# Gated cross-attention and mixture of experts on one core: new step lists, shifts on VectorE, experts by pairs of token tiles

## The reference

```python
def xattn(q, kv):                       # Wq 256x1024, Wk and Wv 128x1024, Wo 1024x256
    qh, kh, vh = heads(q @ Wq), heads(kv @ Wk), heads(kv @ Wv)
    attn = softmax(einsum('bhnd,bhmd->bhnm', qh, kh) * 64 ** -0.5)
    return merge(einsum('bhnm,bhmd->bhnd', attn, vh)) @ Wo + bo

def ffn(x):
    probs = softmax(x @ gate_w.T)       # 8 experts
    comb = the two largest of probs, zero elsewhere
    return sum over e of (x @ expert_w[e].T + expert_b[e]) * comb[:, e:e + 1]

x = x + tanh(g_xattn) * xattn(layernorm(x), ctx)
x = x + tanh(g_ffn) * ffn(layernorm(x))
```

## Time and profile before

| | us |
|---|---|
| median of three runs | 1087.82 (1087.06 to 1088.49) |
| profiled execution, its own time | 1084.83 |
| its span, first to last instruction | 1083.0 |
| start up to the first maximum | 27.7 |
| first batch | 138.4 |
| six middle batches together | 753.6 |
| last batch and tail | 163.3 |

### The profile page before, as it was taken

How to read it: one execution, slowest core, us unless ns; L and a number is a source line. 1 busy time by engine, 2 the same in 40 slices (tenths; PEclk the granted TensorE clock), 3 DMA queues, 4 the chain that set the end, 5 groups by cost and what they waited for, 6 DMA issues and landing times.

```text
span 1083.0 us, 27288 instructions
## 1 busy us (share of the span) xinstructions
PE 950.4 (88%) x10660; PEld 590.7 (55%) x10660; DVE 828.2 (76%) x1551; ACT 788.8 (73%) x1092; POOL 723.0 (67%) x692
## 2 busy tenths in 40 slices
PE   5767669998998989899898989989898989989998
PEld 4245436655655555565465546555555655555583
DVE  5855647797787967799677968879777986778857
ACT  3678869885898848886698848988588866988620
POOL 3479967866677756867478666777578674787510
PEclk7788989999999989999899989999999999999999
DMA  5568759987798849999498956989599985989720
GB/s 166 153 116 136 136 104 181 166 145 120 121 192 158 155 75 170 151 168 153 78 189 158 151 109 124 188 154 159 84 169 166 160 140 97 183 139 152 134 50 20
DMA packets 549135, 150.87 MB, mean 139 GB/s; under 512 B 537592, under 2 KB 547216, under 8 KB 548752
## 3 DMA queue, kind: packets, MB, share of 16 engines
q1 hardware_dynamic: 549008, 149.13, 78.9%
HBM read 11.70 MB, written 4.19 MB: 15 GB/s over the span
## 4 chain that ended last, share of the span: by engine, by line
POOL 33%; issue 19%; PE 17%; ACT 15%; DVE 13%; DMA 1%; SPq 1%; POOLq 0%; ACTq 0%; DVEq 0%
POOL p_s L584 22%; PE MB L1174 9%; ACT pf L741 6%; ACT p_s L751 5%; DVE nmax L903 4%; PE PV L1337 3%; POOL shifts L575 3%; PE ST L1313 3%; POOL xn L559 2%; POOL x L598 2%; PE MB L1186 2%; DVE acc L861 1%; POOL rstd L542 1%; DVE v_s L895 1%; ACT v_s L673 1%
## 5 line engine op out<-in xcount | busy, mean ns | idle before, releaser
L584 POOL TENSOR_TENSOR p_s<-pf,p_s 128x1024 f16<-128x1024 f32 x254 | 541.5, 2132 | 173.2 <-ACT p_s L751 137.6
L741 ACT ACTIVATE pf<-ST,shifts,s_mul 128x512 f32<-128x512 f32 x512 | 370.7, 778 | 152.0 <-POOL shifts L575 150.8
L903 DVE TENSOR_REDUCE nmax<-ST 128x2 f32<-128x1024 f32 x256 | 309.0, 1216 | 38.8 <-PE ST L1313 36.6
L751 ACT ACTIVATE p_s<-pf 128x1024 f16<-128x1024 f32 x254 | 267.6, 1060 | 3.8
L1337 PEld LDWEIGHTS PV<-v_s,pt_s 128*128 128x128 f16 x6096 | 205.9, 98 | 83.9 <-issue 77.7
L1337 PE MATMUL PV<-v_s,pt_s 128*128 128x65 f16 x6096 | 230.2, 194 | 6.0 <-DVE o_n L921 6.0
L1174 PE MATMUL MB<-ex_s,x2t_s 128*128 128x512 f16 x708 | 179.7, 393 | 0.0
L1313 PE MATMUL ST<-KH,QH 64*128 64x512 f16 x512 | 101.2, 391 | 66.3 <-ACT pf L741 54.7
L575 POOL TENSOR_SCALAR shifts<-nmax,s_mul 128x2 f32<-128x2 f32 x256 | 69.4, 271 | 121.4 <-DVE nmax L903 104.3
L861 DVE SCALAR_TENSOR_TENSOR acc<-MB,m,acc 128x256 f32<-128x256 f32 x236 | 113.8, 482 | 24.2 <-PE MB L1174 17.1
L1174 PEld LDWEIGHTS MB<-ex_s,x2t_s 128*128 128x128 f16 x708 | 67.1, 101 | 73.2 <-issue 10.3
(11 more groups left out here) (156 smaller groups left out, 1035.5 us busy)
## 6 DMA issues: line engine op xcount, KB each, us to landing
pt_s<-p_s SPq DMA_TRANSPOSE x508, 3.3
xin<-x SPq DMA_DIRECT2D x7, 512.0 KB, 4.3
out<-acc SPq DMA_DIRECT2D x7, 512.0 KB, 3.7
kvin<-kv_t SPq DMA_DIRECT2D x8, 256.0 KB, 4.2
stage_e<-expert_t SPq DMA_DIRECT2D x1, 2048.0 KB, 10.1
stage_o<-wo SPq DMA_DIRECT2D x1, 1024.0 KB, 5.6
stage_q<-wq SPq DMA_DIRECT2D x1, 768.0 KB, 6.8
xin<-x SPq DMA_DIRECT2D x2, 256.0 KB, 2.8
```

Source lines behind the costliest of these rows:

```text
L584: pool.tensor_tensor(p_s[:, slot, 1, :, :], pf[:, u % 2, :, :], p_s[:, slot, 0, :, :], ALU.subtract).then_inc(p_lo, 1)
L741: last = act.activation(pf[:, u % 2, i, :], ST[u % 2][:, i, :], ACT.Exp, bias=shifts[:, u % 2, i:i + 1], scale=s_mul[:, b % 2:b % 2 + 1])
L751: act.activation(p_s[:, it.ring(p, u, P_SLOTS), 0, :, :], pf[:, u % 2, :, :], ACT.Copy).then_inc(p_hi, 1)
L903: dve.tensor_reduce(nmax[:, t % 2, :], ST[t % 2][:, :, :], AX.X, ALU.max, negate=True)\
```

## The change

1. **Step lists.** All four tables are new. The excerpt of the diff shows GpSimd's; three places follow below as the built programs have them.
2. **Shift on VectorE.** `shift_of` moves from GpSimd's queue into VectorE's, and `DVE_ORDER` gets a `shift` entry for each unit. In 18 of 32 steps it stands straight behind a `maximum`, in 14 behind takes or other work.
3. **Experts by pairs.** An `expert(t, e)` job (one token tile, two experts, 6 matmuls of 512 columns) becomes `pair(j, e)` (two token tiles, one expert, 12 matmuls of 256 columns). There are sixteen of either. VectorE's two additions go to two different tiles of `acc`. The tail keeps the old form.
4. **Late weights.** GpSimd no longer scales or subtracts them: ScalarE copies with the scale, VectorE multiplies and subtracts in one instruction, twelve times in the first batch, steps 10 to 21.
5. **Places.** `pf` has 3 in place of 2, `p_s` 4 in place of 3, `pt_s` 8 in place of 6. So an exponential waits for the `low` of three units before, and a transpose into `pt_s` for the values of eight units before.

```diff
-PF_SLOTS, P_SLOTS, PT_SLOTS = 2, 3, 6
+PF_SLOTS, P_SLOTS, PT_SLOTS = 3, 4, 8
...
-LATE_MAX, LATE_SUM, LATE_AT, LATE_HI, LATE_LO = 2, 5, 7, 1, 2
+LATE_MAX, LATE_SUM, LATE_AT, LATE_HI, LATE_LO = 2, 5, 7, 1, 3
...
 POOL_ORDER = (
-    "shift low", "shift low", "shift low", "shift low", "shift low", "shift low", "shift low", "shift low",
...
-    "shift low", "shift low", "shift low", "shift low", "shift low power1 norm1", "shift low context", "shift low",
...
+    "low", "low", "low", "low", "low", "low", "low", "low", "power2 low", "norm2 low", "low", "residual low", "low",
+    "hold1 low", "low", "hold3 hold2 low", "low", "low", "low", "low", "power1 norm1 low", "low", "low", "low",
+    "context low", "low", "low", "low", "low", "low", "low", "low",
...
-                    raw, of = late[h][0], late[h][3]
-                    pool.tensor_scalar(raw, raw, late_mul[:, of:of + 1], 1.0, ALU.mult, ALU.mult)\
-                        .then_inc(late_scaled, 1)
...
-                    act.wait_ge(late_scaled, h + 1)
-                    act.activation(late[h][1], late[h][0], ACT.Copy).then_inc(late_hi, 1)
+                    of = late[h][3]
+                    act.activation(late[h][1], late[h][0], ACT.Copy, scale=late_mul[:, of:of + 1]).then_inc(late_hi, 1)
...
+                elif kind == "pair":
+                    _, j, e = name
+                    before = it.pair_before(name)
+                    if before is None:
+                        dve.wait_ge(comb_ready, it.b)
+                    elif before[0] == "pair":
+                        dve.wait_ge(pair_half, it.pairs_done(before))
+                    else:
+                        dve.wait_ge(job_free, it.done(JOBS, before) + BANKS)
+                    for i in range(2):
+                        if i == 1 and before is not None:
+                            dve.wait_ge(job_free, it.done(JOBS, before) + BANKS)
+                        t = 2 * j + i
+                        last = dve.scalar_tensor_tensor(acc[:, t, :], m[:, DIM * i:DIM * (i + 1)],
+                                                        comb[:, t, e:e + 1], acc[:, t, :], ALU.mult, ALU.add)
+                        if i == 0:
+                            last.then_inc(pair_half, 1)
...
+            def shift_of(b, p, t):
+
+                dve.wait_ge(max_done, unit_count(b, p, t))
+                dve.tensor_scalar(shifts[:, t % 2, :], nmax[:, t % 2, :], s_mul[:, b % 2:b % 2 + 1], P_SHIFT,
+                                  ALU.mult, ALU.add).then_inc(shift_ready, 1)
...
+                    raw, hi, lo, of = late[h]
+                    dve.wait_ge(late_hi, h + 1)
+                    dve.scalar_tensor_tensor(lo, raw, late_mul[:, of:of + 1], hi, ALU.mult, ALU.subtract)\
+                       .then_inc(late_lo, 1)
...
+                elif kind == "pair":
+                    _, j, e = name
+                    cols = slice(e * DIM, (e + 1) * DIM)
+                    for i in range(2):
+                        q = tile(2 * j + i)
+                        last = parts(m[:, DIM * i:DIM * (i + 1)], [((x2t_s[:, 0, c, q], x2t_s[:, 1, c, q]),
+                                                                    (ex_s[:, 0, c, cols], ex_s[:, 1, c, cols]))
+                                                                   for c in range(LC)])
```

121 lines of the change are left out of this document (64 added, 57 removed), and 3 rows, old and new, of the table PE_ORDER.

## The result

The changed kernel takes **1137.6 us** (median of 4 runs, 1136.9 to 1143.3) against 1087.4 us of the kernel before on the same chip (1085.0 to 1088.5): a ratio of 1.048, 95% interval 1.044 to 1.051. It is slower by 50 us where 68 us less were forecast, and far outside the range of 994 to 1062 us. The profiled execution is the slowest of the four, 1143.3 us. At the end of the study stands a kernel that keeps the whole change, writes its shift as two instructions in place of one and places one step of the first batch later: 999.6 us.

What follows compares the result with a forecast made beforehand. The prediction took TensorE, 91% busy in the middle batches, as the bound. Six middle batches (-47.4 us), the first (-19) and the last (-1.5) summed to -68 us, giving 1020 us, range 994 to 1062.

Steps and rivals of the forecast that it cites:

- I take 0.15: Cost of one shift on VectorE: 0.15 us, between 0.08 and 0.28, plus 0.12 of own wait in 18 of 32 steps.
- no 2.12 us subtraction can stand before it: Shift in VectorE's queue: it follows its maximum, so GpSimd's 2.12 us subtraction no longer delays it.
- VectorE becomes the bound: Rival for the middle batches: at 0.28 us a shift VectorE is busy 109.6 us a batch; 1051 us, chance 0.12.
- slower rival: Rival: in 14 steps shifts come late behind takes in VectorE's queue and TensorE stands; 1111 us, chance 0.06.
- the new lists bring waits of their own: Rival: other 3 us waits with half clock appear elsewhere, a batch gains only 2 us; 1064 us, chance 0.06.
- Context wait and half clock, -6.4 us: Middle batch: TensorE's 3.9 us wait for the context's low part goes, with 2.5 us of half clock behind it.
- Waits for exponentials, -3.5: Middle batch: of TensorE's 5.0 us of waits for exponentials, 3.5 go through the moved shift and added places.
- +2.0 for VectorE's lost slack: Middle batch: VectorE, with 12 us idle in place of 25.5, makes TensorE wait 2.0 us more.
- Pairs: Experts in a middle batch: VectorE's additions save 1.6 us; the doubled weight loads on TensorE cost nothing.
- Waits that cost about 0.1 us: VectorE: an instruction's own wait on the one before costs about 0.1 us, against the skill's rule that it is free.
- First batch, -19: First batch: 19 us less, between 8 and 27, from context wait, half clock and half the waits for exponentials.
- Last batch, -1.5: Last batch: 3.5 us less waiting for exponentials, 2.0 more for VectorE, no context wait; 1.5 us less.

Runs made afterwards that it cites:

- E5: The changed kernel with each shift on VectorE written as two one-element instructions in place of one of two elements: 1009.3 us.
- E2: The changed kernel with the shift made by ScalarE, right ahead of its exponentials, in place of VectorE: 1034.5 us.
- E13: The changed kernel with the shift back on GpSimd, one unit further ahead than in the kernel before: 1039.9 us.
- E6: The kernel before with only the shift moved from GpSimd to ScalarE, old lists and places kept: 1103.7 us.
- E9: The kernel before with only the shift moved from GpSimd to VectorE, as two one-element instructions: 1106.2 us.
- E10: E5 with VectorE's twelve subtractions of late weights in the first batch placed one step later: 999.6 us.
- E3: The kernel before with only the shift moved to VectorE, as one two-element instruction with an immediate constant: 1182.8 us.

## Why the prediction was wrong

- **The step that failed** is the cost of the shift on VectorE: "I take 0.15", bounds 0.08 and 0.28, from two rows. Measured 0.87 us, 223.6 us in the run. The step behind it failed as well: "no 2.12 us subtraction can stand before it". None stands before it in its own queue, but it waits for the one that GpSimd is running. The number was right for an instruction that meets nobody: in the changed kernel, with GpSimd idle, one shift starts at 449.75 and the next instruction at 449.89, 0.14 us later. It was wrong as a bound, since neither row had GpSimd at work beside it, while GpSimd was busy 70% of a middle batch. 32 x (0.87 - 0.15) = 23 us a batch covers VectorE's surplus of 20.6 us over the forecast 105.5. Both signs that the prediction named for this came: VectorE is busy 126.1 of 132.1 us (95%), and TensorE stands 3.26 us for one of its takes. The lower bound came from a reciprocal, and that form does not wait at all: 166 ns, in seven of eight cases in the changed kernel with GpSimd at work.
- **The rival "VectorE becomes the bound"** named the engine that decided, but priced it at 0.28 us a shift and 1051 us. The slower rival (shifts late behind takes, 1111 us) was the wrong mechanism: shifts are late by themselves, and the takes behind them with them. Rival "the new lists bring waits of their own": not borne out for the lists by themselves, as E5's batch has 1.0 us of waits in all.
- **Context wait and half clock, -6.4 us**: right. No wait for kv_s is left in a middle batch of the changed kernel, E2 or E5, and the clock is 1.00 in the latter two. In the changed kernel it is 0.98, since stops of 3.3 us come elsewhere: behind the one that ends at 480.14 us the granted clock is 0.65 on average from 480 to 483 us.
- **Waits for exponentials, -3.5**: 5.0 to 0.8 in E5, -4.2; 3.8 in E2, where ScalarE makes the shift. Right in size for a shift that passes, but put down mainly to the shift: E13, with the shift on GpSimd and the new lists and places, has 1.3. With the old lists the same moves (E6, E9) made it slower.
- **+2.0 for VectorE's lost slack**: not there. In E5 VectorE at 107 of 113.4 us leaves TensorE 1.1 us of gaps. With the other terms a batch comes to 125.6 - 6.4 - 4.2 - 1.5 of small waits = 113.5, and E5 has 113.6. That the forecast 117.7 is E2's 117.6 is luck: E2 has the shift on another engine, and the two terms that were off, +2.0 and the waits for exponentials, offset each other there.
- **Pairs**: right in both halves, -1.8 us on VectorE for -1.6, and no cost of the loads. The rule that loads overlap only when the row group differs (TensorE: Matmul & The Clock Gate, The mechanism, in the Trainium skill) is not borne out for this shape: 22.8 us against 22.7.
- **Waits that cost about 0.1 us**: the doubled halves show it again, 1.8 us in 16 jobs.
- **First batch, -19**: missed by 20 us in E5 and by 11 in E10. The context wait of 8.3 us is gone (no such row in E5 or the changed kernel); the waits for exponentials, of which half was to go, were 19.1 and are 22.2 us in E5. The term left out was VectorE's queue: a wait for ScalarE with a maximum behind it. The subtractions were taken as at most 0.82 us and were 1.49.
- **Last batch, -1.5**: 161.3 us with the tail in E5 against 163.3, so -2.0; in the changed kernel 179.7, +16.4, with the slow shift in it.
- **The range** failed with the bound: with 0.87 us a shift VectorE alone is 105.5 + 23 = 128.5 us busy, more than a whole batch took before (125.6), and the sign turns without any further step. A bound from rows holds only where the rows have the same form and the same neighbour.

## What to carry to other kernels

Before an instruction moves to VectorE, ask what GpSimd does at that moment, and look in the trace for the same kind of instruction under a GpSimd instruction: a small one that ends just behind GpSimd's tells the price. A `tensor_scalar` from SBUF to SBUF of two or three elements waits for it, and so does a `tensor_tensor` with both inputs in SBUF, of one element too. A `tensor_scalar` of one element, a reciprocal (0.17 us) or a maximum over PSUM (1.21 us, both with GpSimd at work and idle) did not here, so a tiny `tensor_scalar` can be split for some 0.1 us. And when a change bundles a good layout with one bad instruction, take them apart before judging: here the same lists went from 5% slower to 7% faster (E5).

## What the runs showed that I had not expected

- A shift of 128x2 elements waits out GpSimd's running instruction, and where the next one follows at once, that too: up to 4.13 us in the changed kernel and 6.64 us in E3. It ends 18 to 32 ns behind it. GpSimd pays nothing for the shifts: its subtraction is 2136 ns on average in the changed kernel and 2138 in E5. It can lose to a longer one: at 94.94 us, 0.07 us behind the start of a late weight's subtraction on VectorE, its own lasts 2.67 us, the longest in the run.
- Two one-element instructions (0.25 us together) are cheaper than one two-element instruction under GpSimd, and dearer by 0.11 us than one with GpSimd idle.
- A `tensor_tensor` with two inputs in SBUF waits for GpSimd even with one element per partition: 1.90 to 1.95 us in seven of eight cases, 0.16 us in the eighth.
- ScalarE makes the same shift in 387 ns whatever GpSimd does.
